# Rotary halves copied by ScalarE and multiplied by GpSimd, in place of a second projection, from the third batch on

## The reference, cut to what matters

```python
def _L1_attn_ref(x, w_qkv, w_out):            # x (8, 512, 128), 16 heads of 8
    qkv = x @ w_qkv
    q, k, v = jnp.split(qkv, 3, axis=-1)      # then to heads
    q = _apply_rope(q, cos, sin)              # [x1*cos - x2*sin, x2*cos + x1*sin]
    k = _apply_rope(k, cos, sin)
    scores = jnp.einsum('bhqd,bhkd->bhqk', q, k) * scale
    scores = jnp.where(causal, scores, jnp.finfo(scores.dtype).min)
    attn = jax.nn.softmax(scores, axis=-1)
    out = jnp.einsum('bhqk,bhkd->bhqd', attn, v)
    return out.transpose(0, 2, 1, 3).reshape(B, S, D) @ w_out
```

## Time and profile before

| | |
|---|---|
| median of 3 runs | 1021.38 us (1018.67 to 1024.7) |
| the profiled execution | 1019.88 us, its span 1018.1 us |
| TensorE's granted clock, mean | 0.873 of full speed |
| attention, from the first row maxima to the last sums | about 544 to 890 us of the span |
| one body of attention, batches in full flow | 41.3 us |

### The profile page before, as it was taken

How to read it: one execution, slowest core, us unless ns; L and a number is a source line. 1 busy time by engine, 2 the same in 40 slices (tenths; PEclk the granted TensorE clock), 3 DMA queues, 4 the chain that set the end, 5 groups by cost and what they waited for, 6 DMA issues and landing times.

```text
span 1018.1 us, 18871 instructions
## 1 busy us (share of the span) xinstructions
PE 785.0 (77%) x5628; PEld 515.3 (51%) x5628; DVE 686.9 (67%) x2470; ACT 511.8 (50%) x1378; POOL 429.0 (42%) x497
## 2 busy tenths in 40 slices
PE   4689883898399960599757888988989898829977
PEld 3578772547297750377632323333433333317757
DVE  4565554775855539855497777888888898576644
ACT  5323331606143323866311466767767677777660
POOL 1047772400177762311176466466484533252100
PEclk9999997895599995799885678989989899969999
DMA  6831113002011122000032332242222300000002
GB/s 152 229 85 49 51 48 96 1 1 83 11 47 51 49 45 72 0 1 1 1 51 35 53 52 41 26 65 30 38 48 30 52 4 3 2 1 0 2 1 84
DMA packets 53428, 42.97 MB, mean 42 GB/s; under 512 B 9862, under 2 KB 48723, under 8 KB 53329
## 3 DMA queue, kind: packets, MB, share of 16 engines
q1 hardware_dynamic: 46784, 31.74, 15.6%
q0 software_dynamic: 4992, 9.32, 3.5%
q10 hardware_dynamic: 1552, 0.70, 0.3%
HBM read 18.27 MB, written 11.40 MB: 29 GB/s over the span
## 4 chain that ended last, share of the span: by engine, by line
PE 43%; DVE 20%; issue 12%; ACT 11%; POOL 7%; DMA 4%; ACTq 1%; DVEq 1%; SPq 0%; POOLq 0%
PE psum L1488 7%; POOL arena L823 5%; PE psum L1473 4%; PE psum L1428 3%; ACT arena L1646 3%; PE psum L1259 3%; PE psum L740 3%; PE psum L1222 2%; PE psum L1231 2%; DVE half_stats L441 2%; PE psum L1460 2%; DVE cst L1553 2%; DVE x L690 2%; POOL result_rows L831 2%; PE psum L1322 2%
## 5 line engine op out<-in xcount | busy, mean ns | idle before, releaser
L1553 DVE CUSTOM_DVE_ANT_0 cst<-psum,rot 128x512 bf16<-128x512 f32 (+3 forms) x512 | 222.7, 486 | 53.1 <-PE psum L1460 47.7
L1646 ACT ACTIVATE arena<-psum 128x512 f32<-128x512 f32 (+1 forms) x384 | 177.9, 533 | 60.7 <-PE psum L1473 54.2
L823 POOL DMA_INDIRECT arena<-xhat_rows,gather_row x78 | 76.9, 985 | 154.5 <-DVE scatter_row L640 131.4
L1460 PE MATMUL psum<-arena 48*128 48x512 bf16 (+3 forms) x512 | 122.7, 332 | 16.8 <-DVE row_max L1553 15.6
L1473 PE MATMUL psum<-arena 51*128 51x512 bf16 (+3 forms) x512 | 113.2, 316 | 11.7 <-ACT arena L1646 8.0
L1737 POOL TENSOR_SCALAR_AFFINE_SELECT arena<-arena 128x384 f32<-128x384 f32 x128 | 63.9, 524 | 127.4 <-ACT arena L1646 127.3
L1488 PE MATMUL psum<-arena 128*32 128x512 f32 (+3 forms) x1024 | 101.1, 494 | 1.9 <-POOL arena L1740 1.9
L831 POOL DMA_INDIRECT result_rows<-arena,scatter_row x78 | 78.3, 1004 | 29.6 <-issue 21.7
L790 PE MATMUL psum<-arena 128*128 x624 | 89.4, 286 | 0.0
L778 PE MATMUL psum<-arena 128*128 128x128 f32 x624 | 86.7, 284 | 1.4 <-DVE arena L652 1.3
L711 ACT ACTIVATE arena<-psum,gate_b1T 128x128 f32<-128x128 f32 x156 | 48.9, 364 | 64.5 <-PE psum L778 64.5
(11 more groups left out here) (249 smaller groups left out, 1689.2 us busy)
## 6 DMA issues: line engine op xcount, KB each, us to landing
arena<-cut SPq DMA_DIRECT2D x192, 64.0 KB
xhat_rows<-xh SPq DMA_DIRECT2D x16, 256.0 KB, 2.3
arena<-result_rows SPq DMA_DIRECT2D x8, 512.0 KB, 6.2
x<-in_L_attn_x SPq DMA_DIRECT2D x4, 512.0 KB, 7.4
arena<-in_L_ffn_w SPq DMA_DIRECT2D x1, 2048.0 KB, 10.3
out<-x SPq DMA_DIRECT2D x4, 512.0 KB, 3.2
arena<-xhat_rows,gather_row POOLq DMA_INDIRECT x78, 2.6
result_rows<-arena,scatter_row POOLq DMA_INDIRECT x78, 2.3
```

Of the source, the lines that this page charges most:

```text
L823: pool.indirect_dma_start(xg[:, j % AHEAD, :], None, xhat_dram, bass.IndirectOffsetOnAxis(gather_row[:, j:j + 1], 0)).then_inc(gathered[j ...
L1460: mm = pe.matmul(to[:, col:col + (k + 1) * P], q_stack[b % STACKS][rows, h, k * P:k * P + P], k_stack[b % STACKS][rows, h, 0:(k + 1) * P], ...
L1553: last = nc.vector.tensor_tensor_reduce(masked_scores[:, number % 2, col:col + n_keys], frm[:, col:col + n_keys], mask[:, S - n_keys:], 1. ...
L1646: nc.scalar.activation(prob_e[g % 2][:, j, first:last], bank[MAX_BANKS + number % EXP_BANKS][:, 0:last - first], ACT.Exp, scale=DH ** -0.5 ...
```

## The change

From batch 2 on the jobs `s0` and `s1` are gone from PE's and DVE's lists, and `p1` moves from slot 13 to slot 12. ACT gets a function `exchange`: after its work of slots 12, 13, 14 and 15 of body `i` it copies one group of 32 partitions of the queries' `raw` to the neighbouring group in `swapped`, and in slots 0 to 3 of body `i+1` the same for the keys, eight copies of 32x512 for each batch. POOL multiplies `swapped` by the sine itself, one 128x512 instruction more in `rotate`, ahead of the cosine, and waits for all four copies before it. POOL's list is also written in another order: the seven instructions for the queries stand in one piece between `causal(i, 0)` and `causal(i, 1)`; those for the keys stand four between pairs 3 and 4 and three between pairs 4 and 5. Batches 0 and 1 are prepared as before.

```diff
@@ JOBS
                 else:
-                    at_body, at_slot = (b - 2,) * 5, (10, 11, 12, 13, 14)
+                    at_body, at_slot = (b - 2,) * 5, (10, 11, 11, 12, 12)
                 for step, i, slot in zip(steps_in, at_body, at_slot):
-                    JOBS[i].append((slot, step, b))
+                    if b < 2 or step[0] != "s":
+                        JOBS[i].append((slot, step, b))
@@ scalar
+                def exchange(b, r, q):
+
+                    nc.scalar.copy(swapped[32 * (q ^ 1):32 * (q ^ 1) + 32, r, :], raw[32 * q:32 * q + 32, r, :]).then_inc(halves_in[r], 1)
+
...
                         for step, b, m in jobs_at(i, hh):
                             job(step, b, m)
+                        at = H * i + hh - 12
+                        if at >= 0 and at % H < 8 and at // H + 2 < B:
+                            exchange(at // H + 2, at % H // 4, at % 4)
@@ gpsimd
                     if i:
-                        causal(i - 1, 1)
+                        for pair in range(1, 4):
+                            causal(i - 1, pair)
                     if keys_next:
-                        rotate(pool, pool, i + 1, 1, 0, 2)
+                        rotate(pool, pool, i + 1, 1, 0, 3)
                     if i:
-                        causal(i - 1, 2)
+                        causal(i - 1, 4)
                     if keys_next:
-                        rotate(pool, pool, i + 1, 1, 2, 4)
+                        rotate(pool, pool, i + 1, 1, 3, 6)
                     if i:
-                        causal(i - 1, 3)
-                    if keys_next:
-                        rotate(pool, pool, i + 1, 1, 4, 6)
-                    if i:
-                        for pair in range(4, PAIRS):
+                        for pair in range(5, PAIRS):
                             causal(i - 1, pair)
-                    if i + 2 < B:
-                        rotate(pool, pool, i + 2, 0, 0, 3)
                     if i < B:
                         causal(i, 0)
                     if i + 2 < B:
-                        rotate(pool, pool, i + 2, 0, 3, 6)
+                        rotate(pool, pool, i + 2, 0, 0, 6)
@@ rotate
                         engine.wait_ge(raw_in[m], b + 1)
+                        if b >= 2:
+                            engine.wait_ge(halves_in[m], 4 * (b - 1))
+                            issue.tensor_tensor(w, w, sin, ALU.mult).then_inc(sines[m], 1)
                         issue.tensor_tensor(v, v, cos, ALU.mult).then_inc(turned_in[m], 1)
```

More of the change, by code:

```diff
@@ L1339, in attention @@
             raw_in = [sem(f"a{n}_raw_in{i}") for i in range(2)]
+            halves_in = [sem(f"a{n}_halves_in{i}") for i in range(2)]
             stack_in = [sem(f"a{n}_stack_in{i}") for i in range(2)]
```

## The result

| | before | after |
|---|---|---|
| median | 1021.15 us (1018.67 to 1024.7, 4 runs) | 1066.37 us (1063.08 to 1068.96, 4 runs) |
| ratio | | 1.0449, 95% interval 1.0421 to 1.0478 |
| span of the profiled execution | 1018.1 us | 1061.3 us |

What follows compares the result with a forecast made beforehand. No engine is full; PE, DVE and ACT hand over PSUM banks, and the latest stops the others. 1019.88 + 36.5 (later sums) + 1.8 (DMAs) = 1058.2; with the median-based 1059.7, 1059 us was taken, range 1047 to 1071.

Steps and rivals of the forecast that it cites:

- The mechanism: At the sums over pairs 0 and 1: GpSimd's queries' train waits for ACT's fourth copy, making pair 1's mask late.
- When the fourth copy ends: ACT's list from slot 12: the fourth queries' copy ends at 707.1, with each copy taken at 0.50 us.
- rival D: ACT's copies across partitions cost 0.77 us each, 1.4 us a place more, 8 in all: 1067 us; chance 0.08.
- the low end of the range: The forecast's own terms with copies and product at their low ends and no DMA term: 1059 - 6 x 1.4 = 1051 us.
- The train: GpSimd's queries' instructions before pair 1: sine product 1.25 us plus cosine and five behind it 7.66 us.
- The shift of the sums: At the end of bodies 1 to 5, sums start at 717.4 against 711.48: 5.9 us later, five times.
- The first place: Body 0 into body 1: sums at 595.6 against 588.63, 7.0 us later, once.
- What comes behind the sums: Maxima's rows and queries' parts on the DMAs: 0.3 us at each of six places, 1.8 us in all.
- The thin margin before pair 5: Keys' train on GpSimd makes pair 5 some 1.6 us later, leaving 1.0 us before the sums at 732.61; no cost.
- TensorE's clock: At the sums' restart: already at half clock before the change, so the longer idle adds nothing.
- VectorE against GpSimd: In slots 0 and 1, each of four cut DVE steps may wait for GpSimd; all end before 717.4, costing nothing.
- Rival A: At the sums, masks are in time and six places gain 1.9 us each: 1010 us; chance 0.07.

Runs made afterwards that it cites:

- pair 1 first: Changed kernel with GpSimd masking pair 1 before the queries' train and SP's list put in the order things become ready: 1020.5 us, 0.9998 of before.
- the rows sooner: As pair 1 first, with the maxima's rows of the first half between the keys' first part and other two in SP's list: 1015.2 us, 0.9936 of before.
- the keys' copies later: As the rows sooner, with the keys' four copies in slots 2 to 5 instead of 0 to 3: 1022.9 and 1024.3 us, 1.0026 of before.

## Why the prediction was right, point by point

*The mechanism.* Pair 1 stands behind the queries' train, the train behind ACT's fourth copy, PE's slot 2 behind the sums. The chain is there in the profile (8.64 us of idle PE, ended by the select; 3.74 us of idle POOL, ended by L1683). It was tested at each link: pair 1 ahead of the train takes the wait for the masks away, and with SP's list in the fitting order all of the loss; an earlier fourth copy takes 3.2 us a place and a shorter train 1.2; and the order without the late start costs nothing that the times tell.

*When the fourth copy ends.* Forecast 9.7 us after the queries' `raw` (707.1 - 697.38); it ended after 10.06, and the train began after 10.21 (730.21 - 720.00). The main mis-sized term is the copy: 0.50 was taken between bounds of 0.30 and 0.77, and it is 0.52 to 0.64, in all 0.3 us more. The copy of the sums took 0.63 for 0.47, and the hand-over to GpSimd, 0.15, was not in the sum. The prediction also has a slip: rival D and the low end of the range count five copies a place, and the path has four. With four D would be 1065 or 1066 us and the low end 1052; neither decides anything here.

*The train* was forecast at 8.91 us and took 8.81; pair 1 was given 1.36 and took 1.4. The shift of the sums was forecast at 5.9 us and was 6.33.

*The first place* was forecast at 7.0 and was 4.9. I had left the exponentials of slot 12 where `s0` had put them, but without it PE gives them sooner: the keys' `raw` starts at 575.97, and I had 578.57. Together, 4.9 + 5 x 6.33 = 36.5 us, exactly the 7.0 + 5 x 5.9 of the forecast; two errors of size cancelled, which is luck.

*What comes behind the sums* was forecast at 1.8 us in all, for DMAs. The span grew by 43.2, so it was 6.7. Nearly all of it lies between the sums and the next queries' `raw`: these five stretches are 2.8, 1.2, 1.1, 0.8 and 0.7 us longer than before, as here 768.29 - 740.43 = 27.86 in place of 738.53 - 711.48 = 27.05. The waits of PE for the maxima's rows in them are 1.39, 0.78, 0.20 and 0.37, in all 2.7 us, of which 1.8 had been expected. A fifth wait, 0.77 behind the last stall, adds nothing to the end: from the sixth sums on the kernel is late by the same 43 us to its last instruction. The other 4 us were not separated. In the same stretches ACT has copies for the keys, which I had costed at nothing. The run without copies shows that ACT's time is not free in another order (0.19 us a copy, queries' and keys' together), so "nothing" was probably too little; no run leaves out the keys' copies alone, and the cause of the 4 us stays open.

*The thin margin before pair 5* held: pair 5 ends at 761.38 and the sums of the third group begin at 762.12, so 0.7 us are left where 1.0 had been expected. In other orders the third group does wait: about 0.5 us with pair 1 first and with the rows sooner, about 0.7 without the copies, and 2.7 with the keys' copies later.

*TensorE's clock.* Before and after, the restart is at half clock: eight entries of sums take 1.93 at 711.48 and 1.94 at 740.43, and the clock is 0.52 and 0.55 in the windows behind the earlier trace rows. The longer idle did not make the restart dearer by much: 5.6 us at 0.55 against 4.5 us at 0.52, some 0.4 us. So the sum could leave the clock out, as it did.

*VectorE against GpSimd.* Each of four small steps "may wait so"; one did, the last, with 0.93 us at 730.61, and three took 0.18 or 0.19, for the maxima came 2 us earlier and GpSimd was idle then. It cost nothing, as forecast. The next four lie beside the keys' train, and two of them took 1.08 and 0.73. So VectorE is 5.3 us less busy and not the forecast 8: the 12 products are gone (8.3), and the small steps take 2.3 more.

*Rival A*, faster, failed by its own condition: the fourth copy would have had to be done before the keys' `raw`. But what speaks for it, the room on ACT and GpSimd, is there: in an order that fits, the same work takes 1011 us. That this is near A's 1010 is no proof of A's sum, since the new order is not A's.

## What to carry to other kernels

Before work goes to an engine with idle time, look at what stands behind it in that engine's list and by when that is due: here the margin was 2.0 us at one place, and the move needed 8.3. Put what others wait for ahead of what can be late, on the engine and in the DMA queue alike, and price the start of a train by its last input, not by its length. If a move of work loses, try it again with the lists in the order in which things become ready, before dropping it: the same 48 copies and 12 products stand in a kernel of 1066 us and in one of 1011. And run the old work in the new order too, or the gain cannot be put down to the move.

## What the runs showed of the hardware that was not expected

A ScalarE copy of 32x512 f32 within SBUF, to other partitions, takes 0.616 us; one of 128x512 from PSUM takes 0.58 to 0.60. A quarter of the partitions saves nothing that shows. With the same source the trace of before shows it too: 24x512 from PSUM takes 0.575, and 128x512 takes 0.590 (the types differ, bf16 and f32).

```profile
L1666 ACT COPY arena<-psum 24x512 bf16<-24x512 bf16 x16 | 9.2, 575 | 24.6 <-PE psum L1436 24.6
L1658 ACT COPY raw<-psum 128x512 f32<-128x512 f32 x16 | 9.4, 590 | 19.6 <-PE psum L1428 19.6
```

So the source in SBUF and the other group of partitions add no more than 0.03 us together.
